# Cross attention: the weighted values right behind the scores of two steps, before the turning

## What is computed

```python
qh = _split_heads(q @ Wq.T + bq)
kh = _split_heads(k @ Wk.T + bk)
vh = _split_heads(v @ Wv.T + bv)
score = jnp.einsum('bhqd,bhkd->bhqk', qh, kh) / jnp.sqrt(jnp.float32(D_K))
attn = jax.nn.softmax(score, axis=-1)
out = jnp.einsum('bhqk,bhkd->bhqd', attn, vh)
out = out.transpose(0, 2, 1, 3).reshape(B, S, H * Dk)
return out @ Wo.T + bo
```

## Time and profile before

| what | value |
|---|---|
| median of 3 runs | 4177.87 us |
| the runs | 4178.8, 4175.75, 4177.87 us |
| profiled execution, its own time | 4171.85 us |
| its span | 4170.5 us |
| mean granted clock of TensorE | 0.951 |

### The profile page before, as it was taken

How to read it: one execution, slowest core, us unless ns; L and a number is a source line. 1 busy time by engine, 2 the same in 40 slices (tenths; PEclk the granted TensorE clock), 3 DMA queues, 4 the chain that set the end, 5 groups by cost and what they waited for, 6 DMA issues and landing times. The chain is left out here.

```text
span 4170.5 us, 102428 instructions
## 1 busy us (share of the span) xinstructions
PE 3803.9 (91%) x42956; PEld 3192.5 (77%) x42956; DVE 2811.9 (67%) x7243; ACT 2135.9 (51%) x2963; POOL 1597.8 (38%) x1647
## 2 busy tenths in 40 slices
PE   7999999854999999988999999986997999999866
PEld 6888888633888888857788888865996888888656
DVE  5777777676777777753777777755446777777544
ACT  4555555442555556533445454533654555555434
POOL 3444343201332332130666655513773333322146
PEclk9999999986999999998999999986998999999968
DMA  3122123001111111010211111102542111110035
GB/s 95 49 65 57 49 65 109 17 23 35 41 41 33 38 44 33 10 39 31 69 53 53 49 64 52 30 12 91 186 148 75 38 33 41 41 33 25 13 104 176
DMA packets 125594, 235.94 MB, mean 57 GB/s; under 512 B 9920, under 2 KB 114768, under 8 KB 121296
## 3 DMA queue, kind: packets, MB, share of 16 engines
q1 hardware_dynamic: 117744, 172.34, 13.9%
q0 software_dynamic: 7392, 57.06, 3.8%
HBM read 208.39 MB, written 20.97 MB: 55 GB/s over the span
## 5 line engine op out<-in xcount | busy, mean ns | idle before, releaser
L599 ACT COPY prob_t<-ps 128x1024 f32<-128x1024 f32 x512 | 518.4, 1013 | 1162.3 <-PE ps L486 1162.3
L486 PE MATMUL ps<-c_ident,prob 128*128 128x128 f32 (+1 forms) x6656 | 916.3, 279 | 12.7 <-ACT prob L737 9.9
L486 PEld LDWEIGHTS ps<-c_ident,prob 128*128 128x128 f32 (+1 forms) x6656 | 717.4, 141 | 188.9 <-issue 157.5
L737 ACT ACTIVATE prob<-prob,nmx 128x1601 f32<-128x1601 f32 x512 | 828.7, 1625 | 1.1 <-DVE nmx L650 1.1
L502 PE MATMUL ps<-ctx,wk 128*128 128x400 f32 (+1 forms) x3072 | 691.7, 361 | 21.9 <-DVE vals L609 14.1
L516 PE MATMUL ps<-wv,ctx 128*128 128x256 f32 x4992 | 704.4, 289 | 3.3 <-DVE vals L609 3.1
L516 PEld LDWEIGHTS ps<-wv,ctx 128*128 128x128 f32 x4992 | 619.9, 186 | 10.5 <-DVE vals L609 4.0
L641 DVE CUSTOM_DVE_ANT_0 prob<-ps,mk 128x400 f32<-128x400 f32 (+2 forms) x1024 | 526.2, 569 | 112.9 <-PE ps L474 110.4
L644 DVE TENSOR_SCALAR_CACHE_REDUCE prob<-ps 128x400 f32<-128x400 f32 (+2 forms) x1024 | 526.1, 569 | 90.9 <-PE ps L474 90.7
L502 PEld LDWEIGHTS ps<-ctx,wk 128*128 128x128 f32 x3072 | 534.8, 191 | 45.3 <-DVE vals L609 28.5
L599 DVE COPY prob_t<-ps 128x1024 f32<-128x1024 f32 (+1 forms) x384 | 402.3, 1048 | 239.1 <-PE ps L486 238.8
(11 more groups left out here) (350 smaller groups left out, 4313.0 us busy)
## 6 DMA issues: line engine op xcount, KB each, us to landing
raw_ctx<-in_ctx_t SPq DMA_DIRECT2D x120, 400.0 KB, 3.3
raw_ctx<-in_ctx_t SPq DMA_DIRECT2D x60, 402.0 KB, 5.1
raw_ctx<-in_ctx_t SPq DMA_DIRECT2D x60, 399.0 KB, 3.3
mk<-in_mask_f SPq DMA_DIRECT2D x32, 400.2 KB, 5.5
mk<-in_mask_i SPq DMA_DIRECT2D x16, 800.5 KB, 4.4
sorted<-zeros SPq DMA_DIRECT2D x2, 3840.0 KB, 20.6
rows<-sorted SPq DMA_DIRECT2D x30, 256.0 KB, 5.2
done<-done SPq DMA_DIRECT2D x30, 256.0 KB, 2.5
```

What stands on the lines that cost most here:

```text
L486: mm = pe.transpose(ps[0:w, turn_bank(u, i) + a, r * P:(r + 1) * P], prob[u % 2][:, r, x * P:x * P + w], cst['ident'][:])
L599: copy(prob_t[0:w, ring(u, i), 0:nb, :], ps[0:w, turn_bank(u, i):turn_bank(u, i) + nb, :]).then_inc(st[sem], 1)
L737: a.activation(prob[h % 2][:, r, :], prob[h % 2][:, r, :], ACT.Exp, bias=nmx[:, r:r + 1], accum_out=den[h % 2][:, r:r + 1]).then_inc(st['e ...
```

## The change

`WEIGHTED_AT` said that PE weights the steps 0 and 1 at the end of step 2 and the steps 2 and 3 at the end of step 4, behind the keys. Now it weights 0, 1 and 2 in step 3, between the scores and the turning. The steps 3, 4, 5 and 6 (before: 4, 5, 6) go over to the next half (`CARRIED`), where they stand with the denominators between the scores and the turning of step 0, no longer behind the keys.

The turned probabilities of step 6 have a buffer of their own, `last_t`, and the four places of `prob_t` go round over 6 steps of a half rather than over 7, which changes what a copy waits for. For the space, the output weights `wout` lie in the first of the two buffers of the raw context, and SP loads them at the end of the stage, behind the last context transfer, rather than at its start. No other engine's code is moved.

```diff
--- before.py
+++ after.py
@@ -299,7 +299,9 @@
 CH = len(KCH)
 TURNED, HEADS, UNIT = 4, 6, 7
 LAST = HALVES - 1
-WEIGHTED_AT = {2: (0, 1), 4: (2, 3)}
+WEIGHTED_AT = {3: (0, 1, 2)}
+CARRIED = (3, 4, 5, 6)
+RING = 4
 
 def cross_attention(k, L, scale, mask=None, wo='Wo', bo='bo'):
 
@@ -312,12 +314,12 @@
     raw_ctx = [st.tile(f"raw_ctx{i}", [P, C, KCH[0][1]]) for i in range(2)]
     ctx = st.tile("ctx", [P, 2, C, KEYS2], F32R)
     keys = [st.tile(f"keys{g}", [P, 2, KEYS2], F32R) for g in range(2)]
-    wout = st.tile("wout", [P, C, D])
+    wout = raw_ctx[0][:, :, 0:D]
     mk = [st.tile(f"mk{i}", [P, KEYS]) for i in range(2)] if mask else None
     kept = st.tile("kept", [P, KEYS]) if mask == 'fill' else None
     vals = [st.tile(f"vals{i}", [P, KT, D]) for i in range(2)]
     prob = [st.tile(f"prob{i}", [P, ROWS, KEYS]) for i in range(2)]
-    prob_t = st.tile("prob_t", [P, 4, 2, 512])
+    prob_t, last_t = st.tile("prob_t", [P, RING, 2, 512]), st.tile("last_t", [P, 1, 512])
     q_heads = st.tile("q_heads", [P, C, P])
     q_parts = [st.tile(f"q_parts{i}", [P, 2, C, P], F32R) for i in range(2)]
     mx = st.tile("mx", [P, ROWS, CH])
@@ -426,8 +428,9 @@
 
         return [t for t in ([i - 1] if u == LAST - 1 else [i + 5]) if 0 <= t < T - 1 and (u < LAST or i == 1)]
 
-    def ring(u, i):
-        return (u * STEPS + i) % 4
+    def turned(u, i):
+
+        return last_t if i == STEPS - 1 else prob_t[:, (u * (STEPS - 1) + i) % RING]
 
     def sp():
         sp = nc.sync
@@ -437,7 +440,6 @@
         sp.dma_start(first_ctx[:, :, columns(3)], ctx_chunk(0, 3)).then_inc(st['first3'], 16)
         if mask:
             load_mask(0)
-        sp.dma_start(wout[:], by_rows(dram[name + wo])).then_inc(st['wout'], 16)
         sp.dma_start(k.row[:], dram['bias_rows'][BIAS_ROWS.index(name + bo)].partition_broadcast(P)).then_inc(st['row'], 16)
         for b in range(1, B):
             if mask:
@@ -448,6 +450,8 @@
                 if b > 1 or i >= 2:
                     sp.wait_ge(*st.at('ctx_lo', CH * b + i - 1))
                 sp.dma_start(raw_ctx[i % 2][:, :, 0:width(i)], ctx_chunk(b, i)).then_inc(st[f'ctx{i % 2}'], 16)
+        sp.wait_ge(*st.at('ctx_lo', CH * B - 1))
+        sp.dma_start(wout, by_rows(dram[name + wo])).then_inc(st['wout'], 16)
         if L == 0:
             clear_sorted(k, st, zeros)
 
@@ -530,7 +534,7 @@
                 for r in range(ROWS):
                     mm = pe.matmul(ps[32 * r:32 * r + 32, HEADS, g * P:(g + 1) * P],
                                    vals[b % 2][0:w, x, (ROWS * g + r) * 32:(ROWS * g + r + 1) * 32],
-                                   prob_t[0:w, ring(u, i), a, r * P:(r + 1) * P], start=(x == 0), stop=(x == KT - 1))
+                                   turned(u, i)[0:w, a, r * P:(r + 1) * P], start=(x == 0), stop=(x == KT - 1))
             mm.then_inc(st['pv_mm'], 1)
 
         def spread_denominators(u):
@@ -568,7 +572,13 @@
         for u, i, attend, score, chunk, pairs in steps():
             if score:
                 scores(u + 1, i)
+            if u >= 1 and i == 0:
+                for x in CARRIED:
+                    weighted(u - 1, x)
+                spread_denominators(u - 1)
             if attend:
+                for x in WEIGHTED_AT.get(i, ()):
+                    weighted(u, x)
                 turn(u, i)
             if 6 in pairs:
                 make_values(u // 2 + 1, 6)
@@ -581,14 +591,7 @@
             if u >= LAST - 1:
                 for t in out_tiles(u, i):
                     project_out(t)
-            if attend:
-                for x in WEIGHTED_AT.get(i, ()):
-                    weighted(u, x)
-            if u >= 1 and i == 0:
-                for x in (4, 5, 6):
-                    weighted(u - 1, x)
-                spread_denominators(u - 1)
-        for x in (4, 5, 6):
+        for x in CARRIED:
             weighted(LAST, x)
         spread_denominators(LAST)
         project_out(T - 1)
@@ -596,13 +599,17 @@
     def turned_copy(copy, sem, u, i):
 
         w, nb = rows_of(blocks(i)[-1]), len(blocks(i))
-        copy(prob_t[0:w, ring(u, i), 0:nb, :], ps[0:w, turn_bank(u, i):turn_bank(u, i) + nb, :]).then_inc(st[sem], 1)
+        copy(turned(u, i)[0:w, 0:nb, :], ps[0:w, turn_bank(u, i):turn_bank(u, i) + nb, :]).then_inc(st[sem], 1)
 
     def turned_ready(engine, u, i):
-        n = u * STEPS + i
-        engine.wait_ge(*st.at('t_mm', n + 1))
-        if n >= 4:
-            engine.wait_ge(*st.at('pv_mm', n - 3))
+        n = u * (STEPS - 1) + i
+        engine.wait_ge(*st.at('t_mm', u * STEPS + i + 1))
+        if i == STEPS - 1:
+            if u:
+                engine.wait_ge(*st.at('pv_mm', u * STEPS))
+        elif n >= RING:
+            old_u, old_i = divmod(n - RING, STEPS - 1)
+            engine.wait_ge(*st.at('pv_mm', old_u * STEPS + old_i + 1))
 
     def values_copy(copy, sem, b, n):
         w, nb = rows_of(blocks(n)[-1]), len(blocks(n))
```

## The result

| | before | after |
|---|---|---|
| median | 4176.9 us (4 runs) | 4385.64 us (4 runs, 4383.03 to 4393.39) |
| profiled execution, own time | 4171.85 us | 4385.01 us |
| span | 4170.5 us | 4383.7 us |
| mean granted clock | 0.951 | 0.945 |

The change makes the kernel slower, by a ratio of 1.0507 (95% interval 1.0491 to 1.0523), 209 us. The forecast was 4365, with a range of 4305 to 4405. One execution of the kernel before, of 5338 us at a granted clock of 0.71, stood among the 13 beside the first four experiments, and the ratios leave it out.

What follows compares the result with a forecast made beforehand. PE was taken to bound the kernel, with DVE only just in time. Three stages' 167 and the fill stage's 21 made 188 on 4171.85, so 4360; the runs' median, 6 above, gave 4365 us, range 4305 to 4405.

Steps and rivals of the forecast that it cites:

- The bound: Whole kernel: PE is busy for 91% of the span, and DVE has no spare time in front of step 2's scores.
- The fixed cost of a block, 0.13: PE's weighting blocks: each costs 0.13 us besides its matmuls, so the change as such saves 0.13 in each half.
- S before W as before T: PE's scores before weighting cost what they cost before turning, 0.75 us; bounds 0.13 less or more.
- K0 at 3.50: Step 0's keys on PE start 3.50 us after its scores, before 1.61, as weighting and denominators of 1.89 precede them.
- T2 hanging on K0: Step 2's turning follows step 0's keys through DVE's queue: later by 1.68 us in even halves, 1.89 in odd.
- POOL in the odd halves: DVE's `XNT` ends just behind POOL's tensor_tensor, so odd halves keep 7.16 us from step 0's keys to step 2's turning.
- T2 to V5, +0.13: Step 2's turning to step 5's values: 0.53 us later at step 3's weighting, 0.40 earlier behind step 4's keys.
- The fill stage: Stage where DVE reads keys without ACT: even halves -0.13 us, odd halves +1.54, 21 for the stage.
- The buffers at nothing: The moved `wout` load, `last_t` and the ring of `prob_t` places cost nothing.
- PE's clock falls: Rival: PE's waits bring the granted clock to 0.95 over four stages, 135 us more, 4500; 6 in 100.
- a slower signal: Bound: the signal before step 5's values may take 0.2 us instead of 0.05, 17 us more.
- The tiling rule: Changes of tiling mode on PE drop from 12 to 10 a half; at 0.13 each, 30 us gained over 116 halves.

Runs made afterwards that it cites:

- the first four experiments: e1, e2, e3 and e8, run beside the kernel before at a median of 4173.17 us.
- e1: Changed kernel, with DVE's three `outputs` instructions moved in front of `keys_low` of step 0's keys: 4210.62 us, 1.0096 of the kernel before.
- e6: Kernel before, with only DVE's three `outputs` instructions moved from the end of step 0 to behind `largest` of chunk 1: 4128.28 us, ratio 0.9894.
- e2: Kernel before, with only the weighting of steps 4, 5, 6 and the denominators moved in front of step 0's turning: 4301.41 us, ratio 1.0312.
- e3: Changed kernel, with the carried weighting (steps 3 to 6) and denominators back behind step 0's keys: 4218.70 us, 1.0104 of the kernel before.
- e4: Changed kernel, with the weighting of step 2 behind step 4's keys instead of in step 3: 4318.36 us, 1.0347 of the kernel before.
- e7: Changed kernel, with POOL's first context part of an odd half held until DVE's three `outputs` are done: 4324.17 us, 1.0365 of the kernel before.
- e8: Changed kernel's buffers, copy waits and late `wout` load, with PE's order of the kernel before: 4170.49 us, 1.0003 of the kernel before.

## Why the prediction was right

**The bound.** PE is the bound, and DVE is only just in time: right. e1 shows it, where DVE's order alone gives some 170 us back, the clock's 30 among them, and e6, where the same in the kernel before gives 43. PE's busy time, though, was to stay within 1% and grew by 3.8%: the forecast left out that the rows of matmuls take in their waits.

**The fixed cost of a block, 0.13, and S before W as before T.** Right: S0 took 0.76 before W, and the block with 56 + 8 matmuls 405.13 - 403.24 = 1.89 (from the timeline of the same half). That scores next to weighting would cost by themselves is refuted.

**K0 at 3.50, and T2 hanging on K0.** Right: 3.50; K0 to T2 6.33 in even halves (forecast 6.51) and 7.19 in odd ones (7.16), with T2 2.86 after `largest`. e2, which has this part alone, cost 128 of the forecast 137. The even halves' 6.51 was too high by 0.18: DVE gets from K0 to `rmask` in 2.56 (before 2.86) and from `rmask` to `largest` in 0.91 (before 1.00), and the forecast took off only 0.21. The 2.85 from `largest` of chunk 1 to T2 held: in the even and odd halves of the add and the fill stage the median is 2.84 to 2.87 in the changed kernel, in e2, e3, e4 and e7.

**POOL in the odd halves.** Right, and now shown: e7 holds POOL's instruction back and `XNT` is short.

**T2 to V5, +0.13.** Right: T2 to T3 4.41 (4.42), K2 to V5 2.77 (2.75). e4 shows the wait for bank 7 by filling it. The waits in S2 came out wider than the 1.3 to 1.8 of the forecast: from V1 to T2 it is 3.46 in even halves and 4.32 in odd ones, of which V1 and S2 themselves take 2.24, so PE waits 1.2 and 2.1.

**The fill stage.** Its sum was 21; measured by the distances of S0 (halves 1 to 29) it is 23. Within it the odd halves are as forecast (+1.54), and an even half was 0.27 short (+0.14 for -0.13), since it took K0 and not the mask instruction beside POOL to decide there.

**The buffers at nothing.** Right, by e8.

**The clock.** Here the forecast chose wrongly in part. "PE's clock falls" stood among the rivals with 6 in 100, at 135 us for all four stages (of some 2700 us; their stretches add up to 3003, which would make it 150). It did fall, but in 21 halves and for 30 us. The argument that the fill stage keeps 1.00 with a wait of over a microsecond was true of the fill stage and said too little of the others. By the distances of S0 in halves 1 to 29, the three stages grew by some 63 each, 10 of these by the clock; the remaining 53 were forecast as 55.6. So 3 x 53 + 23 + 30 = 212, and the span grew by 213. Without the clock the forecast of 188 would have been 6 too high; with it, 25 too low. The time lies in the range because the upper bound had 47 us in it for S before W and for a slower signal, and neither cost anything: 0.76 and 0.05. That the room held the clock's 30 is luck. Had all odd halves but the last of each stage fallen, 21 more, it would have been some 30 more, 4416 by this estimate and outside the range.

**The tiling rule.** The Trainium skill, "TensorEngine Tiling (Array Packing)", Key Properties, says that a change of the tiling mode drains TensorE. By it the new order, with two changes fewer in a half, should have gained. The trace agrees in so far as a block has a fixed cost: 0.13 for the one that is saved, 15 us over 116 halves, less than a tenth of what the waits cost. That this 0.13 is a drain, no run here shows.

## What to carry to other kernels

When a block is moved on the engine that bounds the kernel, look at what it stood beside: it was cover for another engine's work, and here the cover was worth more than the block. Then ask which instructions stand in the other engine's queue behind the one that gets late, whether they need it or not; moving three small ones that don't was worth 43 us in the kernel before. And a wait added on an engine with slack (POOL here, e7) can make the whole faster, where it keeps that engine's instruction from running beside one that the bound engine waits for. Last, a mean over a stage can hide what happens in single halves: count the distances from block to block.

## What the runs showed of the hardware

**The clock can fall after a wait of some 2 us, and does not always.** In the changed kernel PE stood, in odd halves, from the end of V1 (about 434.5) until DVE released the last bank for S2 (about 436.4), with only a few matmuls in between, and then ran at 1.2 GHz for some 3.4 us, in 21 of 45 halves. The Trainium skill, "TensorE: Matmul & The Clock Gate", Why this matters for your kernels, warns that an idle gap of PE between bursts of matmuls can bring the clock down. The trace agrees, and shows it with a gap of under 2 us, shorter than those that the page warns of; there the measurement decides. It is not the length of the wait alone: e4 and e2 have the same wait in their odd halves (T2 7.18 and 7.19 after K0), and the clock fell in 7 and in 1 of their 45. With the wait shorter by some 0.86 it fell in none (e7), and in none of the even halves either. Why some odd halves fall and others not is open.

**`XNT`, a DVE instruction with two inputs in SBUF, waits until POOL's instruction has ended.** It takes 0.28 alone, and 0.82 or 1.16 when POOL's tensor_tensor began before it. In the changed kernel all 71 of the long ones end 0.08 to 0.09 us behind a tensor_tensor of POOL, and in e6 42 of 57 do so behind a cast of POOL. The two instructions before it, which read PSUM, never took more than 0.29 in any of the runs, beside the same POOL instruction too. But DVE's mask instruction, with one input in SBUF, got longer as well, from 0.98 to 1.39 in the fill stage.
